# A long convolution on one Trainium2 core: 36 pair columns a batch instead of 40, at a step of 64 columns in PSUM

## The reference

```python
x = x + attention(layernorm(x))
x = x + xattn(ctx, ctx, layernorm(x), ssm_kernel, D, head_dim=8)
x = x + ffn(layernorm(x))

def xattn(k, v, q, ssm_kernel, D, head_dim):      # here k is v: both are the context
    # B = 8, L = 512 is the axis that is convolved, 256 = H * head_dim, so H = 32
    k_, v_, q_ = (a.reshape(B, H, head_dim, L) for a in (k, v, q))
    kv = einsum('bhil,bhjl->bijhl', k_, v_)        # 8 x 8 products of rows i and j of one head
    y = irfft(rfft(kv, n=2 * L) * rfft(ssm_kernel, n=2 * L))[..., :L]   # causal convolution with the head's taps
    out = y + kv * D
    return einsum('bijhl,bhil->bjhl', out, q_)     # contraction over i
```

## Time and profile before

| | before |
|---|---|
| time, median of 3 runs | 1668.42 us |
| time of the profiled execution | 1668.36 us |
| its span, first to last instruction | 1666.1 us |
| TensorE busy | 1491.5 us (90%) |
| VectorE busy | 791.2 us (47%) |
| ScalarE busy | 671.7 us (40%) |
| GpSimd busy | 856.9 us (51%) |
| mean granted TensorE clock | 0.933 of 2.4 GHz |

### The profile page before, as it was taken

How to read it: one execution, slowest core, us unless ns; L and a number is a source line. 1 busy time by engine, 2 the same in 40 slices (tenths; PEclk the granted TensorE clock), 3 DMA queues, 4 the chain that set the end, 5 groups by cost and what they waited for, 6 DMA issues and landing times. The chain is left out here.

```text
span 1666.1 us, 28412 instructions
## 1 busy us (share of the span) xinstructions
PE 1491.5 (90%) x7766; PEld 1141.7 (69%) x7767; DVE 791.2 (47%) x1093; ACT 671.7 (40%) x1823; POOL 856.9 (51%) x924
## 2 busy tenths in 40 slices
PE   3899999599996814899999999999999999999965
PEld 1455555367774814788888888888888888888852
DVE  3366564458888376625617443474472552000003
ACT  0555555323331220344444544544444444444420
POOL 2444554044441042567767766766776766665530
PEclk9999999789997555899999999999999999999987
DMA  6000000032325331625435444454452542421115
GB/s 238 3 1 0 0 0 1 1 88 83 88 88 186 131 107 27 189 72 130 119 76 145 115 107 100 104 161 100 109 157 68 138 108 62 120 50 31 31 19 215
DMA packets 77787, 148.59 MB, mean 89 GB/s; under 512 B 9152, under 2 KB 13760, under 8 KB 77760
## 3 DMA queue, kind: packets, MB, share of 16 engines
q1 hardware_dynamic: 61536, 110.36, 21.5%
q0 software_dynamic: 14544, 35.92, 10.9%
q10 hardware_dynamic: 1680, 1.97, 0.4%
HBM read 115.38 MB, written 32.85 MB: 89 GB/s over the span
## 5 line engine op out<-in xcount | busy, mean ns | idle before, releaser
L1445 PE MATMUL ps_h<-w_hi,xh 128*128 x720 | 254.7, 365 | 1.4 <-ACT xh L1371 1.4
L1446 PE MATMUL ps_h<-w_lo,xh 128*128 x720 | 250.1, 358 | 0.0
L1468 PE MATMUL ps_y<-w_hi,hh 128*128 x600 | 243.2, 405 | 4.4 <-issue 4.4
L1278 DVE TENSOR_TENSOR w_lo<-stage,w_hi 128x512 f32 x220 | 231.1, 1050 | 27.0
L1469 PE MATMUL ps_y<-w_lo,hh 128*128 x600 | 237.2, 395 | 0.0
L1324 POOL TENSOR_TENSOR y<-y,b_sb 128x512 f32<-128x512 f32 x60 | 80.9, 1349 | 235.1 <-ACT y L1396 235.1
L1317 POOL TENSOR_TENSOR hl<-h,hh 128x1280 fp32r<-128x1280 f32 x60 | 192.7, 3211 | 13.6 <-ACT hh L1390 13.5
L758 PE MATMUL ps_b<-kv,toe 128*128 128x320 f32 x640 | 174.9, 437 | 7.1 <-DMA toe<-kpad 7.1
L1450 PE MATMUL ps_h<-w_hi,xl 128*128 x720 | 169.6, 357 | 0.0
L1377 ACT ACTIVATE h<-ps_h 128x512 f32<-128x512 f32 x180 | 82.0, 527 | 214.6 <-POOL hl L1317 206.5
L758 PEld LDWEIGHTS ps_b<-kv,toe 128*128 128x128 f32 x640 | 122.9, 192 | 59.0 <-issue 9.0
(11 more groups left out here) (197 smaller groups left out, 2390.3 us busy)
## 6 DMA issues: line engine op xcount, KB each, us to landing
stage<-in_wcat SPq DMA_DIRECT2D x240, 256.0 KB
toe<-kpad SPq DMA_DIRECT2D x32, 256.0 KB, 3.3
cc<-in_ctx_rev SPq DMA_DIRECT2D x32, 192.0 KB, 3.2
acc<-zeros POOLq DMA_DIRECT2D x1, 4352.0 KB, 18.0
xs<-in_x SPq DMA_DIRECT2D x4, 1024.0 KB, 13.2
x2d<-xs SPq DMA_DIRECT2D x4, 1024.0 KB, 8.3
xnd<-xn_c SPq DMA_DIRECT2D x16, 256.0 KB, 2.0
w_hi<-x2d SPq DMA_DIRECT2D x2, 2048.0 KB, 13.0
```

The lines of the kernel that those rows point to most:

```text
L1278: nc.vector.tensor_tensor(lo, stage[:, c % NSTAGE], hi.bitcast(F32), ALU.subtract).then_inc(split_done, 1)
L1445: nc.tensor.matmul(out, x_hi, part(w_hi, e, k * FF + lo, hi - lo), start=(k == 0), stop=False)
L1446: nc.tensor.matmul(out, x_hi, part(w_lo, e, k * FF + lo, hi - lo), start=False, stop=False)
L1468: nc.tensor.matmul(ps_y[:], h_hi, part(w_hi, e, KD * FF + k * D, D), start=(k == 0), stop=False)
```

## The change

The columns of a batch are laid out anew: first the 8 x 4 = 32 near ones (`NEAR`; row i times row i+d, d = 0 to 3), then 4 far ones (`FAR`; row i times row i+4, i = 0 to 3), 36 together (`NPAIR`).

- GpSimd forms them in two instructions instead of one, the far ones (4 blocks x 8 batches x 4 = 128 elements a partition) and then the near ones (1024). The second one signals.
- The matmuls have 8 x 36 = 288 moving columns, which lie together in SBUF. They are written to PSUM as 8 runs of 36 columns at a step of `SPAN` = 64, so that four banks form one regular row of 32 steps.
- ScalarE copies in three instructions: 8 x 4 near columns of three rows in front (384 elements), all near ones (1024), and the far ones (128 read, 256 written, each to rows i and i+4). `ye` has the layout of before.
- VectorE's three instructions, the loads, the waits, the buffers' number and the order of heads are as before.

```diff
+NEAR = CH * (ND - 1)
+FAR = CH // 2
+NPAIR = NEAR + FAR
+SPAN = 512 // B
-        NCOL = B * ND * CH
+        NCOL = B * NPAIR
# multiply
                 nc.gpsimd.tensor_tensor(
-                    view(kv[:, buf], 0, [[ND * CH, LB * B], [ND, CH], [1, ND]]),
-                    view(c, 0, [[CE, LB * B], [1, CH], [0, ND]]),
-                    view(c, 0, [[CE, LB * B], [1, CH], [1, ND]]), ALU.mult).then_inc(kv_ready, 1)
+                    view(kv[:, buf], NEAR, [[NPAIR, LB * B], [1, FAR]]),
+                    view(c, 0, [[CE, LB * B], [1, FAR]]),
+                    view(c, FAR, [[CE, LB * B], [1, FAR]]), ALU.mult)
+                nc.gpsimd.tensor_tensor(
+                    view(kv[:, buf], 0, [[NPAIR, LB * B], [ND - 1, CH], [1, ND - 1]]),
+                    view(c, 0, [[CE, LB * B], [1, CH], [0, ND - 1]]),
+                    view(c, 0, [[CE, LB * B], [1, CH], [1, ND - 1]]), ALU.mult).then_inc(kv_ready, 1)
# evacuate
-                for at, src, n in ((0, (CH - WRAP) * ND, WRAP * ND), (WRAP * ND, 0, CH * ND)):
-                    ins = nc.scalar.activation(
-                        view(ye[:, par], at, [[B * YE, LB], [YE, B], [1, n]]),
-                        view(ps[:], 4 * par * 512 + src, [[512, LB], [CH * ND, B], [1, n]]), ACT.Copy)
-                ins.then_inc(ye_ready, 1)
+                near = ND - 1
+                for at, src, n in ((0, (CH - WRAP) * near, WRAP), (WRAP * ND, 0, CH)):
+                    nc.scalar.activation(
+                        view(ye[:, par], at, [[YE, LB * B], [ND, n], [1, near]]),
+                        view(ps[:], 4 * par * 512 + src, [[SPAN, LB * B], [near, n], [1, near]]), ACT.Copy)
+                nc.scalar.activation(
+                    view(ye[:, par], WRAP * ND + near, [[YE, LB * B], [FAR * ND, 2], [ND, FAR]]),
+                    view(ps[:], 4 * par * 512 + NEAR, [[SPAN, LB * B], [0, 2], [1, FAR]]), ACT.Copy)\
+                    .then_inc(ye_ready, 1)
# convolve
-                        last = nc.tensor.matmul(ps[:, 4 * par + l, 0:NCOL], toe[:, par, (l - m) * P:(l - m + 1) * P],
+                        last = nc.tensor.matmul(view(ps[:], (4 * par + l) * 512, [[SPAN, B], [1, NPAIR]]), toe[:, par, (l - m) * P:(l - m + 1) * P],
```

## The result

The changed kernel takes 1662.67 us (median of 18 runs) beside 1667.47 us for the kernel before (18 runs): ratio 0.9971, 95% interval 0.9964 to 0.9978. It gains 4.8 us where 10.9 were forecast. The direction was right and so was the place to which the bound moved, but the gain is less than half of the forecast.

A forecast was written before the change was run, and what follows sets the result against it. TensorE was taken to bound the kernel before, with VectorE close behind and bounding after the change. Profiled 1668.36 us less 10.4 (31 shorter periods) and 0.5 (first head) gave 1657.5 us, range 1653 to 1664.

The forecast's parts named there:

- The matmuls: TensorE's 20 records a head: 0.2426 us apart instead of 0.2693, 4.85 us a head, 0.53 less, no cost for the step.
- VectorE becomes the bound: VectorE's unchanged 4.86 us plus a gap set a 5.05 us period instead of 5.384, saving 10.4 us; chance 0.65.
- The gap behind the reduce: VectorE's idle time from the reduce's end to the next TT1: 0.19 us, 0.14 plus 0.05 for half a loop end.
- The bound from above: Upper end for VectorE's gap: 0.53 us at every second head's loop end, mean 0.335, period 5.20 us, saving 5.7 us.
- a sign of being wrong: In VectorE's profile, a gap above 0.3 us behind every second reduce would show the loop end was misjudged.
- The first head: Stage start: TensorE's first 20 records, partly at 1.2 GHz, take 0.5 us less and move the first TT1 forward.
- Who waits anew: TensorE catches up with GpSimd's `kv` after some 17 heads, then idles 0.2 us a head; nobody pays, clock stays 1.00.
- the rival: GpSimd's time T bounds through VectorE's products: period at least 2.43 + T; at T 2.78, 1662.4 us; chance 0.14.
- The other two rivals: Matmuls: the PSUM step slows them, up to 1772 us, chance 0.11 slower; or 288 columns save nothing, 1668 us, 0.06.

The follow-up runs named there:

- wait_late: Changed kernel with VectorE's wait for its reduce moved from behind the reduce to in front of the next head's first product: 1655.07 us, ratio 0.9926.
- pool_extra2: Changed kernel with two more GpSimd products of 128 elements a head, into a tile nobody reads: 1674.79 us (one run).
- pool_extra3: Changed kernel with three more GpSimd products of 128 elements a head, into a tile nobody reads: 1686.68 us (one run).
- step_alone: Kernel before, 40 columns a batch kept, with only the step of 64 in PSUM: 1667.84 us, ratio 0.9999.
- turn32: Changed kernel with VectorE's 32 heads written out, no loop on that engine: 1650.89 us, ratio 0.9894.
- before_two_prod: Kernel before with two buffers for VectorE's products, so it waits for the reduce two heads back: 1667.35 us, ratio 0.9997.
- the two edits: Two buffers for VectorE's products, or its 32 heads written out: 1667.35 and 1668.05 us on the kernel before, 1649.26 and 1650.89 on the changed one.

## Why the prediction was wrong, and where it was right

- **The matmuls, right.** 0.2424 us a record against 0.2426 forecast, and no price for the step. The Trainium skill's sentence that any non-contiguous pattern slows matmuls ("PSUM — Partial Sum Buffer", Specifications (TRN2)) does not hold for runs of 40 floats at a step of 64: the ratio is 0.9999.
- **VectorE becomes the bound, right.** From TT1's start to the reduce's end it takes the 4.86 us of the earlier trace rows, unchanged (5.23 - 0.37).
- **The gap behind the reduce, mis-sized: the step that failed.** The forecast took 0.14 us from the gap between TT2 and the reduce and 0.05 as half a loop's end, 0.19 in the mean; the trace has 0.23 and 0.52, 0.37 in the mean. 31 x (0.37 - 0.19) = 5.6 us, of the 6.1 between forecast and result. The nearest row was the wrong one: behind TT2 the queue has a single wait and has done nothing else meanwhile, behind the reduce it had the next head's work before it. The code shows that (`wait_ge(res_ready, h + 1)` stands last in `contract`, the loop's end behind it), and wait_late shows that 0.14 would have been right with the line at the other place. The bound from above, 0.53 us at the loop's end, was nearly the value (0.52), but for the other heads it kept 0.14, where 0.23 was measured, so the measured 5.23 us lies above the bound of 5.20. The prediction named a gap above 0.3 us behind every second reduce as a sign of being wrong, and this is the sign that came.
- **The first head, mis-sized too, by 0.2 us.** Forecast 0.5 us less. From TensorE's first matmul to ScalarE's first copy it takes 7.93 us where it took 8.14. The slow records are 0.480 us apart, as forecast, but the granted clock stayed at 1.2 GHz for 5.4 us of matmuls and not for the 4.9 of before; in the other kernels it is 3.8 to 5.4 us, so this part differs from run to run. Also, ScalarE's three copies take 1.96 instead of 1.73 us, since the far copy of 256 elements takes 648 ns and not 410 (single elements at a step of 5 on the writing side, each read twice). In this execution `toe` was no longer the last to arrive, GpSimd's `kv` was. In all the first TT1 comes 0.27 us earlier (15.16 to 14.89 us after the first issue of `cc`).
- **Who waits anew, right.** TensorE catches up with `kv`, from the tenth to twelfth head on instead of the seventeenth, since VectorE is slower than forecast. The table of waits gives it 2.9 us in 11 waits; that is only what shows behind the last record's 0.41 us. From 345 to 495 us the trace has 587 records, and 587 x 0.2424 = 142.3 us, so about 7.7 of the 150 us are waiting. The clock stays at 1.00, and at the stage's end it idles 11.0 us where 11 were forecast. Nobody pays.
- **GpSimd.** T is 2.30 us against 2.39 forecast (1.89 and 0.45); the rival had the right formula and the wrong size, as pool_extra2 and pool_extra3 show. Its time, 1662.4 us, is 0.3 us from the measured one, but that is chance: TT1 is never longer than 1.53 us, so GpSimd held nothing up.
- **The other two rivals** fall: the step costs nothing (step_alone), and a matmul of 288 columns is shorter (records of 406 ns, 0.2424 us apart, where 320 columns had 432 and 0.2693).

The parts of the gap can be read from the queue. A bare wait costs 0.03 us (turn32, TT2 to the reduce). The register instruction of 57 ns in front of TT1, behind the wait, makes it 0.14 (wait_late). In kernel after one more stands behind the wait for the reduce, the sum of 40 ns for the wait for `ye` (L784, at 422.9 where the reduce ends at 422.88 and TT1 starts at 423.10), which wait_late has in front of it (L786 above): 0.23. The loop's end adds 0.29. The same 0.09 shows where `ye` comes last: TT1 follows it by 0.14 us in kernel before and by 0.23 in before_two_prod, which has a second wait behind the one for `ye`.

## What to carry to other kernels

When a faster engine hands the bound to the next one, cost that one not by its instructions but by its period if nothing else made it wait, and read its queue for what stands behind each wait for its own result. A wait that closes a loop's body holds back the register sums and the branch (here 0.29 us a turn, 0.37 us of 5.23 in the mean), while the same wait at the head of the next round lets them run beside the last instruction. Such costs are invisible as long as another engine bounds, so put an edit that removes them together with the one that uncovers them: alone, each of the two edits was worth nothing on the kernel before, and with the change they are worth 13 and 12 us.

## What the runs showed of the hardware

- A matmul that writes 8 runs of 40 float32 columns at a step of 64 takes as long as one that writes 320 in a row (432 ns records, 5.38 us a head, ratio 0.9999).
- A wait of VectorE for its own last instruction costs 0.14 us in a loop, where one register instruction of 57 ns stands behind it, and 0.03 us where the heads are written out (TT2 to the reduce). One more register instruction behind the wait adds 0.09 us, the end of a loop turn 0.29.
- A VectorE product that meets a GpSimd one ends 1.38 us after that one (pool_extra2), where it takes 1.52 alone; the reduce isn't changed beside one (2285 to 2289 ns in all these kernels, the last heads without a GpSimd product included).
- A ScalarE copy that writes single elements at a step of 5, and reads each of its elements twice, takes 648 ns for 256 elements, where the line through the old copies gives 405. Which of the two costs isn't shown. Runs of 4 cost nothing: 514 and 1037 ns for 384 and 1024 elements are on that line.
